# Scores of four heads as 32-row matmuls on four partition groups, in place of stacked copies of Q and K

## The reference

```
q = layer_norm(x, g1, b1)
qh = (q @ wq + bq).reshape(B, S, 16, 32);  kh, vh likewise from ctx
scores = einsum('bqhd,bkhd->bhqk', qh, kh) / sqrt(32)
scores = where(k <= q, scores, -inf);  probs = softmax(scores)
o = einsum('bhqk,bkhd->bqhd', probs, vh).reshape(B, S, 512)
x1 = x + (o @ wo + bo)
h = layer_norm(x1, g2, b2)
out = x1 + gelu(h @ w1 + b1) @ w2 + b2
```

## Time and profile before

| what | value |
|---|---|
| median of three runs | 3329.34 us (3326.11 to 3329.54) |
| profiled execution, span (its own time is not listed apart) | 3330.8 us |
| attention stage | about 0 to 1825 us |
| feed-forward stage | about 1825 to 3331 us |
| PE, DVE, ACT, POOL busy in the whole span | 91%, 47%, 35%, 13% |
| DMA, mean | 80 GB/s; 512 copies to `stack` of 256 KB each |
| mean granted clock of TensorE | 0.947 of full speed |

### The profile page before, as it was taken

How to read it: one execution, slowest core, us unless ns; L and a number is a source line. 1 busy time by engine, 2 the same in 40 slices (tenths; PEclk the granted TensorE clock), 3 DMA queues, 4 the chain that set the end, 5 groups by cost and what they waited for, 6 DMA issues and landing times. The chain is left out here.

```text
span 3330.8 us, 52513 instructions
## 1 busy us (share of the span) xinstructions
PE 3040.0 (91%) x17576; PEld 2464.2 (74%) x17576; DVE 1564.2 (47%) x4164; ACT 1160.6 (35%) x2958; POOL 418.8 (13%) x368
## 2 busy tenths in 40 slices
PE   5888888888888888888887999999999999999999
PEld 4677677767776777677765788888888888888887
DVE  4665666566656665566654343332223333333222
ACT  2555555555555554555543211111111111111111
POOL 0211221122111211121111120000000000000000
PEclk8899899989998999899988899999999999999999
DMA  6766777667777777777763211110011111111100
GB/s 136 115 113 105 115 123 120 107 104 124 124 109 109 124 123 108 109 124 123 109 104 95 104 39 38 38 38 26 13 37 38 38 38 38 38 38 38 38 25 13
DMA packets 142192, 265.99 MB, mean 80 GB/s; under 512 B 12800, under 2 KB 12800, under 8 KB 142080
## 3 DMA queue, kind: packets, MB, share of 16 engines
q1 hardware_dynamic: 142080, 264.84, 43.1%
HBM read 97.02 MB, written 33.55 MB: 39 GB/s over the span
## 5 line engine op out<-in xcount | busy, mean ns | idle before, releaser
L722 ACT ACTIVATE sm<-sm,mins 128x128 f32<-128x128 f32 (+3 forms) x1024 | 571.8, 559 | 820.3 <-DVE mins L576 817.2
L576 DVE CUSTOM_DVE_ANT_0 sm<-bank_s,mask 128x128 f32<-128x128 f32 (+3 forms) x1024 | 480.5, 488 | 610.6 <-PE bank_s L422 488.7
L1154 ACT ACTIVATE g_sb<-bank_f,b1s 128x512 f32<-128x512 f32 x256 | 176.2, 688 | 1175.0 <-PE bank_f L964 1175.0
L422 PE MATMUL bank_s<-stack 128*128 128x128 f32 (+3 forms) x1024 | 378.4, 413 | 187.4 <-DMA stack<-st_lo 187.4
L1066 DVE CAST g_hi<-g_sb 128x512 fp32r<-128x512 f32 x256 | 112.7, 440 | 869.5 <-ACT g_sb L1154 869.5
L434 PE MATMUL bank_t<-ident,sm 128*128 128x128 f32 x2560 | 444.6, 291 | 30.4 <-DVE pT L517 20.3
L434 PEld LDWEIGHTS bank_t<-ident,sm 128*128 128x128 f32 x2560 | 321.3, 148 | 133.5 <-issue 65.5
L962 PE MATMUL bank_f<-hT_hi,w_hi 128*128 128x512 f32 x1024 | 407.4, 398 | 1.6 <-DVE hT_lo L1060 1.6
L962 PE MATMUL bank_o<-w_hi,g_hi 128*128 128x512 f32 x1024 | 408.5, 399 | 0.0
L964 PE MATMUL bank_f<-hT_hi,w_lo 128*128 128x512 f32 x1024 | 406.9, 397 | 0.0
L964 PE MATMUL bank_o<-w_hi,g_lo 128*128 128x512 f32 x1024 | 406.6, 397 | 0.0
(11 more groups left out here) (108 smaller groups left out, 4464.6 us busy)
## 6 DMA issues: line engine op xcount, KB each, us to landing
stack<-st_hi SPq DMA_DIRECT2D x256, 256.0 KB, 6.4
stack<-st_lo SPq DMA_DIRECT2D x256, 256.0 KB, 8.6
xt<-in_x SPq DMA_DIRECT2D x32, 1024.0 KB, 6.2
c_raw<-in_ctxT SPq DMA_DIRECT2D x64, 256.0 KB, 6.9
x_scratch<-xt SPq DMA_DIRECT2D x64, 256.0 KB, 3.8
xn<-x_scratch SPq DMA_DIRECT2D x16, 1024.0 KB, 7.7
xr<-x_scratch SPq DMA_DIRECT2D x16, 1024.0 KB, 5.6
out<-xr SPq DMA_DIRECT2D x64, 256.0 KB, 2.1
```

The source lines that it names most:

```text
L422: mm = pe.matmul(bank_s[n % BANKS_S][:, off:off + w], stack[:, g % 2, 0, r, P * qt:P * qt + P], stack[:, g % 2, 1, r, 0:w], start=True, st ...
L576: op = V.tensor_tensor_reduce(sm[:, n % SLOTS_S, off:off + w], bank_s[n % BANKS_S][:, off:off + w], mask[:, 512 - w:512], 1.0, 0.0, ALU.ad ...
L722: op = A.activation(row, row, ACT.Exp, bias=mins[:, g % 2, c:c + 1], scale=-1.0, accum_out=sums[:, g % 2, c:c + 1])
L1154: A.activation(g_sb[:, f % 2, :], bank_f[f % 2][:], ACT.Gelu, bias=b1s[:, f:f + 1], scale=1.0).then_inc(gelu, 1)
```

## The change

Q and K keep their natural column order, so that head r of a group has partitions 32r to 32r+31 of `st_hi` and `st_lo`, which now hold two groups (`par`). The copies, `stack` and their semaphore are gone. Scores are made in waves: in every fourth step TensorE makes the scores of four tiles, one for each head, with matmuls of 32 rows; each head writes its own bank (`bank_s[0..3]`), and three partial products (the low by low one is left out) accumulate there. `tile_of` now puts the four heads' query tile 2 into tiles 4 to 7 and query tile 3 into tiles 8 to 11. `softmaxed(n)` spreads the masks and exponentials of a wave over three steps: two, one, one, none. VectorE and ScalarE now do the move before them. The two banks that this takes come from the transposes (one bank instead of two) and the dense jobs (two instead of three). `sm` has 8 slots instead of 4. Q and K jobs that ran over three steps run over two, and X0 to X3 stand in steps 8, 9, 10 and 11.

```diff
-BANKS_S = 2
-BANKS_D = 3
-SLOTS_S = 4
+BANKS_D = 2
+SLOTS_S = 8
@@ tile_of
-    return 1, (k - 4) // 2, (2 + (k - 4) % 2,)
+    return 1, k % 4, (1 + k // 4,)
+def softmaxed(n):
+    return ((n, n + 1), (n + 1,), (n + 1,), ())[n % 4]
@@ BESIDE
-        [("B", {0: 4}), ("Q1", {0: 4, 1: 4, 2: 4}), ("K1", {2: 4, 3: 4, 4: 4}), ("R", {5: 4}), ...
-        [("Q2", {0: 6, 1: 6}), ("K2", {2: 4, 3: 4, 4: 4}), ("R", {4: 4}), ("O1", {5: 12}), ...
-        [("Q3", {0: 4, 1: 4, 2: 4}), ("K3", {2: 4, 3: 4, 4: 4}), ... ("X0", {8: 4}), ("X1", {8: 4}), ("X2", {9: 4}), ("X3", {10: 4})],
+        [("B", {0: 4}), ("Q1", {0: 6, 1: 6}), ("K1", {2: 6, 3: 6}), ("R", {5: 4}), ...
+        [("Q2", {0: 6, 1: 6}), ("K2", {2: 6, 3: 6}), ("R", {4: 4}), ("O1", {5: 12}), ...
+        [("Q3", {0: 6, 1: 6}), ("K3", {2: 6, 3: 6}), ... ("X0", {8: 4}), ("X1", {9: 4}), ("X2", {10: 4}), ("X3", {11: 4})],
@@ buffers
-        st_hi = sb("st_hi", [P, 2, S], F32R)
-        st_lo = sb("st_lo", [P, 2, S], F32R)
-        stack = sb("stack", [P, 2, 2, 4, S], F32R)
+        st_hi = sb("st_hi", [P, 2, 2, S], F32R)
+        st_lo = sb("st_lo", [P, 2, 2, S], F32R)
-        bank_s = [pb(f"bank_s{i}") for i in range(BANKS_S)]
-        bank_t = [pb(f"bank_t{i}") for i in range(2)]
+        bank_s = [pb(f"bank_s{i}") for i in range(4)]
+        bank_t = pb("bank_t")
@@ sync: the copies and their waits go, the stores and loads stay
-                for g in range(2):
-                    stacks(it, g)
-                    if not it.first:
-                        for t in ((0,), (1, 2, 3))[g]:
-                            store(it, t)
+                if not it.first:
+                    for t in range(QT):
+                        store(it, t)
@@ tensor: score
                 if k == 0:
-                    pe.wait_ge(stacked, it.b * (128 * NG) + 128 * (g + 1))
-                pe.wait_ge(masked, it.b * TB + (n + 1))
+                    for job in (f"Q{g}", f"K{g}"):
+                        pe.wait_ge(d_free[it.bank(job, g - 1)], it.bank_read(job, g - 1))
+                if n > 0 or not it.first:
+                    pe.wait_ge(masked, it.b * TB + n)
                 for qt in qts:
                     w = P * (qt + 1)
-                    mm = pe.matmul(bank_s[n % BANKS_S][:, off:off + w], stack[:, g % 2, 0, r, P * qt:P * qt + P],
-                                   stack[:, g % 2, 1, r, 0:w], start=True, stop=True)
+                    for part, (q, k_) in enumerate(((st_hi, st_hi), (st_hi, st_lo), (st_lo, st_hi))):
+                        for r in range(4):
+                            rows = slice(HD * r, HD * r + HD)
+                            mm = pe.matmul(bank_s[r][:, off:off + w], q[rows, par, 0, P * qt:P * qt + P],
+                                           k_[rows, par, 1, 0:w], start=(part == 0), stop=(part == 2))
@@ tensor: p_transpose, pv and the loop
-                pe.wait_ge(moved[n % 2], it.b * (TB // 2) + (n // 2 + 1))
+                pe.wait_ge(moved, it.b * TB + (n + 1))
-                    if not it.tail:
+                    if not it.tail and n % 4 == 0:
                         score(it, n)
@@ vector and scalar loops
-                    if not it.tail:
-                        mask_and_max(it, n)
                     if (n > LAG and ...) and not act_moves((n - LAG - 1) % TG):
                         move_tile(dve, V.tensor_copy, it, n - LAG - 1)
+                    if not it.tail:
+                        for tile in softmaxed(n):
+                            mask_and_max(it, tile)
@@ scalar: qk_high
-                    act.wait_ge(stacked, G * 128)
+                    act.wait_ge(scored, it.b * (TB // 4) + 3 * g)
@@ host
-        "wq": feature_major(w["wq"]),
-        "wk": feature_major(w["wk"]),
+        "wq": w["wq"],
+        "wk": w["wk"],
```

More of the change, by code:

```diff
@@ L166, in stage_a @@
         c_in = [sem(f"c_in{i}") for i in range(2)]
-        stacked = sem("stacked")
         carriers = sem("carriers")
@@ L173, in stage_a @@
             sem(n) for n in ("consts", "bias_mm", "scaled", "w_hi_done", "w_lo_done", "wo_lo_done", "bvx_ok", "bias_ok"))
-        scored, masked, probs, transposed, pv_done = (
-            sem(n) for n in ("scored", "masked", "probs", "transposed", "pv_done"))
-        moved = [sem(f"moved{i}") for i in range(2)]
+        scored, masked, probs, transposed, moved, pv_done = (
+            sem(n) for n in ("scored", "masked", "probs", "transposed", "moved", "pv_done"))
         recip_ok, rexp_ok, o_prod, oT_hi_ok, oT_done = (
@@ L211, in place @@
                 if g < 0:
-                    return {"V0a": -1}[job]
+                    return {"V0a": -1, "K0": -2 if self.first else -3, "Q0": -3 if self.first else -4}[job]
                 return self.order.index((job, g))
@@ L261, in load_c @@
                 sp.dma_start(c_raw[:, fb % 2, :], one(c_v, m)[:, fb, :]).then_inc(c_in[fb % 2], 16)
[L263 to L269, removed]
             sp.sem_inc(stored, 16)
@@ L291, in _ @@
             load_weight(3)
[L292 to L305, removed]
             def store(it, t):
@@ L341, in body @@
                 sp.dma_start(xt[:], one(x_v, b)).then_inc(res_in, 16)
-                if not it.last:
-                    stacks(it, 3)
             over_batches(sp, body)
@@ L431, in p_transpose @@
                 pe.wait_ge(probs, it.b * TB + (n + 1))
-                pe.wait_ge(moved[n % 2], it.b * (TB // 2) + (n // 2 + 1))
+                pe.wait_ge(moved, it.b * TB + (n + 1))
                 for c in range(sum(qt + 1 for qt in qts)):
-                    mm = pe.transpose(bank_t[n % 2][:, P * c:P * c + P], sm[:, n % SLOTS_S, P * c:P * c + P], ident[:])
+                    mm = pe.transpose(bank_t[:, P * c:P * c + P], sm[:, n % SLOTS_S, P * c:P * c + P], ident[:])
                 mm.then_inc(transposed, 1)
@@ L439, in pv @@
                 last_tile = TG * g + (3 if pair == 0 else 11)
-                for i in range(2):
-                    pe.wait_ge(moved[i], it.b * (TB // 2) + ((last_tile + 1) // 2 + 1))
+                pe.wait_ge(moved, it.b * TB + (last_tile + 2))
                 if pair == 0:
@@ L506, in move_tile @@
             eng.wait_ge(pv_done, it.b * (2 * NG) + (2 * g + pair + 1))
-            bank = bank_t[n % 2]
+            bank = bank_t
             if pair == 0:
@@ L516, in move_tile @@
                 src = bank[:, 0:P * (qt + 1)].rearrange("p (c q) -> p c q", q=P)
-            copy(out, src).then_inc(moved[n % 2], 1)
+            copy(out, src).then_inc(moved, 1)
         @block.vector
@@ L559, in qk_low @@
                 w, hg, bank = "QK".index(job[0]), int(job[1]), it.bank(job, g)
+                par = hg % 2
                 dve.wait_ge(qk_hi, G * 2 + (w + 1))
                 bias = bqs[:, hg:hg + 1] if w == 0 else vec[:, 3, hg:hg + 1]
-                V.scalar_tensor_tensor(st_lo[:, w, :], bank_d[bank][:], bias, st_hi[:, w, :].bitcast(F32),
+                V.scalar_tensor_tensor(st_lo[:, par, w, :], bank_d[bank][:], bias, st_hi[:, par, w, :].bitcast(F32),
                                        ALU.add, ALU.subtract).then_inc(d_free[bank], 1)
@@ L586, in o_product @@
                 V.tensor_tensor(rT[:], bank_v[:], rT[:], ALU.mult).then_inc(o_prod, 1)
-            dve.sem_inc(masked, BANKS_S)
             dve.sem_inc(o_prod, 1)
-            for i in range(2):
-                dve.sem_inc(moved[i], 1)
+            dve.sem_inc(moved, 1)
             for i in range(BANKS_D):
@@ L693, in qk_high @@
                 w, hg, bank = "QK".index(job[0]), int(job[1]), it.bank(job, g)
+                par = hg % 2
                 act.wait_ge(dense, it.done(job, g))
-                if it is not pro:
-                    act.wait_ge(stacked, G * 128)
+                if it is not pro and not (it.first and g == 0):
+                    act.wait_ge(scored, it.b * (TB // 4) + 3 * g)
                 bias = bqs[:, hg:hg + 1] if w == 0 else vec[:, 3, hg:hg + 1]
-                A.activation(st_hi[:, w, :], bank_d[bank][:], ACT.Identity, bias=bias,
+                A.activation(st_hi[:, par, w, :], bank_d[bank][:], ACT.Identity, bias=bias,
                              scale=1.0).then_inc(qk_hi, 1)
@@ L715, in exponential @@
                 _, r, qts = tile_of(k)
[L716 removed]
+                act.wait_ge(masked, it.b * TB + (n + 1))
                 off = 0
@@ L756, in body @@
                     g, k = divmod(n, TG)
-                    if not it.tail:
-                        exponential(it, n)
                     if (n > LAG and not it.tail or n <= LAG and not it.first) and act_moves((n - LAG - 1) % TG):
                         move_tile(act, A.copy, it, n - LAG - 1)
+                    if not it.tail:
+                        for tile in softmaxed(n):
+                            exponential(it, tile)
                     if not (it.first and g == 0):
```

19 lines of the change are left out of this document (8 added, 11 removed), and 6 rows, old and new, of the table BESIDE.

## The result

The changed kernel takes 3413.28 us (median of four runs; 3407.98 to 3414.31) against 3328.85 before: a ratio of 1.0248, 95% interval 1.0232 to 1.0263. I had forecast 3187 and a range up to 3320. It is slower by 84 us, and 226 us above the forecast. The profiled execution took 3407.98 us, with a span of 3406.3.

A forecast was written before the change was run, and what follows sets the result against it. TensorE, busy 91% of 3330.8 us, was taken as the bound, lacking stacked copies in attention. Terms sum to -8.0 us per batch, -128 over 16, ends -14: 3331 - 142 - 2 = 3187 us; range for 8 in 10: 3070 to 3320.

The forecast's parts named there:

- step (d): One transpose bank: transposes wait for the move of four tiles earlier; 3.5 us less 1.3 already there, +2.2 a batch.
- What the scores cost: Score matmuls on TensorE: 2.7 us a group after, switches included, against 2.6 before; +0.4 us a batch.
- the switch: TensorE entering and leaving a score wave: 0.10 us each way, three waves, +0.6 us a group.
- the rival by the Trainium skill's 3.07: Score rounds take about 1.3 times as long: +0.6 us per group, some 40 us over the kernel; no chance given.
- (a): The eight copy DMAs per group and TensorE's waits for them go: -11.7 us per middle batch.
- (c): Two dense banks instead of three: O1 waits in group 1, +1.1 us, V1b in group 2, +3.0.
- Q0's 1.6: X3 and its low part slip a step, and Q0 in group 3 needs it: +1.6 us a batch.
- (e): LayerNorm's end: X waits unchanged (0), Q0 late +1.6, one cold stretch stays +1.5 us a batch.
- (b): TensorE's half clock in three stretches a batch behind the copies' waits goes: -6.1 us, of which +1.5 stays.
- The case on the other side: Row groups don't overlap in a group's 48 score matmuls: 7.6 us instead of 2.1, 3459 us in all; chance 0.06.
- weights in series: Score weights load one after another, only multiplying overlaps: 5.3 us a group, 3337 us in all; chance 0.10.
- They chain: A 3 us wait in group 2 lowers the clock, backlog enters group 3: 5 us more a batch, 3267; chance 0.16.

The follow-up runs named there:

- after_pad16: The changed kernel with 16 idle semaphore increments ahead of TensorE's loop, shifting its instructions by 16 places: 3316.51 us (0.9963 of before).
- after_unrolled: The changed kernel with the loop over the 14 middle batches written out, same instructions in the same order: 3307.71 us (0.9932 of before).

## Why the prediction was wrong

**The sign: a term that wasn't there.** The prediction counted 48 matmuls in place of 16 as time of the array alone. It put what 252 more instructions do to a loop body at nothing, without a reason. At the place where the body lies they cost 97 to 106 us (after_pad16, after_unrolled), 7.1 us a batch by the table, and turned a gain of 0.4% into a loss of 2.5%. Without the fetch the change stands at 3316.5 us. That lies just inside my range, but the gain is 12 us and not 142, so it doesn't speak for the rest of the sum.

**The size: step (d), the single transpose bank.** I priced it at 3.5 us a batch by counting steps without other work, and allowed +2.2. In after_pad16 the gaps went from 2.1 to 9.5 us, +7.3, which is 5.1 more than forecast. I had missed that tile 5's move, made in step 9, waits on ScalarE behind the exponentials of tiles 8 and 9, and that each late move pushes the next; how the 5.1 us divide between these isn't shown. The runs show that this term depends on three orders at once: ScalarE's moves, low parts against masks, and where dense work lies.

**What the scores cost.** The rounds are as forecast or better: all four row groups at once, and a middle round starts 0.11, 0.12, 0.17 or 0.23 us after the one before, as a single matmul would, without the 0.02 of stagger that I had added (-1.0 us a batch). What 16 score matmuls cost before is right as well: replaced by what stands between the same neighbours without them, they come to 2.5 us a group against 2.6.

The step that failed here is the switch. I had 0.1 us to enter a wave and 0.1 to leave it. In the lines above it is 1.66 us from the last three transposes to the second dense start (1003.59 to 1005.25), where three transposes, three rounds and one dense matmul need 1.25: 0.41 us, some 0.1 each ahead of the wave, in its first round, in its last and in the first dense matmul. The other waves show the same. Twelve a batch make +2.5 us over my 0.2 each.

By the table score, transposes, P·V and warm excess went from 41.3 to 43.4 us a batch, +2.0 instead of +0.4. The 0.32 us of the first dense matmul behind a transpose (1015.85 to 1016.17) are no loss: the four transposes before it take 0.35 instead of 0.44, which makes up for it. In size the rival by the Trainium skill's 3.07 (TensorE: Matmul & The Clock Gate, Measured speedup vs the span model) came near, with +0.6 us a group against a measured +0.4. But the time lies in the switches: a middle round of 512 columns takes 0.23 us for four matmuls, as long as one.

**Right.** (a): the 11.4 us of copies' waits are gone. (c): the wait for K3's bank is 2.84 us against 3.0, O1's 1.1 against 1.1; st_lo and xnT_lo together make 5.9 us of gaps against 5.7 forecast with Q0's 1.6. (e): X's own waits fell by 1.0 instead of staying. **Missed besides.** Group 2 is 30.0 us long, 3.6 more than before, where I had said about as long as before; groups 0 and 3, which I had 4 to 6 us shorter, are 3.1 and 1.6 shorter in after_pad16. **Half right.** (b): of three half-clock stretches a batch less than one is left in after_pad16, but by the start distances of dense matmuls and transposes the cold excess was only 4.2 us before, not 6.1; 3.2 came back instead of 4.6.

Added up: forecast batch 101.2 us (109.2 by the table, less 8.0), + 5.1 for (d), + 1.6 for the scores, + 1.4 for the clock, + 0.3 for the copies (11.4 instead of 11.7), + 0.2 for the dense bank, - 1.0 for X: 108.8 against 108.9 in after_pad16; and 7.1 for the fetch makes 115.9 against 116.0 in the changed kernel.

Of the rivals none was the one that came. The case on the other side, row groups that don't overlap, was excluded by the trace, and so are weights in series. "They chain" has half of its mechanism in after_pad16: late moves push the next ones, but the clock isn't turned down behind them (cold excess 1.0 us a batch).

## What to carry to other kernels

Count a loop body's instructions on each engine, not only their time, and look at the instruction queue's packets in the page: if they come again in each round, try shifting the body by a few idle instructions before doing anything larger. Where matmuls of another tiling are put in, price the way in and out on both sides of each switch: here that was 0.41 us a wave, twice what I had counted. When a change takes away a bank, its price is set by what stands ahead of the instruction that frees the bank, so order each engine's step by who waits: first what frees a bank, but only where it delays nothing that is itself late. Gains of such orders don't add: two that gave nothing or a loss alone (0 and +25 us) gave 60 us together.

## What the runs showed of the hardware

- Four matmuls of 32 rows on the four row groups, each with its own bank, run at the same time in fp32r, weight loads included: a middle round of 128 columns starts 0.11 us after the one before, one of 512 columns 0.23 us. Going from 128-row matmuls to such a wave and back cost 0.41 us in all.
- A jump back whose target had to be fetched cost TensorE 6.5 us on average (13 times, nine packets of 16 KB in each round); the same body 16 places further cost nothing (31 packets in the whole run instead of 148), and 128 places further 3.4 us.
- Semaphore increments by themselves start 0.15 us apart in TensorE's queue; 64 of them took 9.6 us, during which it did no other work once the matmuls before them had ended.
- Straight code is fetched with little or no visible wait: the changed kernel written out is 9 us faster than with the loop that stays in memory, the kernel before 12 us slower.
